# Two GpSimd sums placed behind both normalisations of a step, and unread TensorE products around the last two second norms, in a four-block sequence model

## What is computed

```python
# layers 0, 1 and 3; layer 1 has a causal mask and no bias on q, k, v
h = layernorm(x) * (1 + scale1) + shift1             # "first norm"
x = x + gate1 * (softmax(q(h) k(h).T / 4) v(h) @ Wo + bo)
h = layernorm(x) * (1 + scale2) + shift2             # "second norm"
x = x + gate2 * (gelu(h @ W1 + b1) @ W2 + b2)
# layer 2: attention, then a second norm added to its own input, no MLP
x = x + (softmax(q k.T) v / 16) @ Wp + bp
x = x + gamma * layernorm(x) + beta
```

## Time and profile before

| | us |
|---|---|
| median of 3 runs | 1178.21 (1176.1 to 1182.58) |
| the profiled execution | 1179.05 |
| its span, first to last instruction | 1177.3 |
| PE busy | 1073.8 (91%) |
| PEld busy | 852.4 (72%) |
| DVE busy | 779.3 (66%) |
| ACT busy | 574.3 (49%) |
| POOL busy | 174.9 (15%) |
| mean granted TensorE clock, full = 1 | 0.981 |

### The profile page before, as it was taken

How to read it: one execution, slowest core, us unless ns; L and a number is a source line. 1 busy time by engine, 2 the same in 40 slices (tenths; PEclk the granted TensorE clock), 3 DMA queues, 4 the chain that set the end, 5 groups by cost and what they waited for, 6 DMA issues and landing times.

```text
span 1177.3 us, 21434 instructions
## 1 busy us (share of the span) xinstructions
PE 1073.8 (91%) x7540; PEld 852.4 (72%) x7540; DVE 779.3 (66%) x2091; ACT 574.3 (49%) x1140; POOL 174.9 (15%) x288
## 2 busy tenths in 40 slices
PE   5799999999999999999999978888888999999895
PEld 4667777788787787877888755555556787877664
DVE  4476667776677666777666677766768766667622
ACT  4245565554553445544456444444445545655441
POOL 3011011110113101101101101111114110101100
PEclk9799999999999999999999999999999999999988
DMA  7732333222345223331233433333434123332200
GB/s 235 252 113 65 92 109 109 81 63 72 109 154 188 67 83 109 109 103 56 70 106 112 136 110 109 109 109 109 132 130 145 56 75 108 117 117 67 78 2 17
DMA packets 102714, 123.20 MB, mean 105 GB/s; under 512 B 8992, under 2 KB 96032, under 8 KB 101600
## 3 DMA queue, kind: packets, MB, share of 16 engines
q1 hardware_dynamic: 102048, 121.73, 33.1%
q10 hardware_dynamic: 576, 0.30, 0.1%
HBM read 85.16 MB, written 35.78 MB: 103 GB/s over the span
## 4 chain that ended last, share of the span: by engine, by line
PE 64%; DVE 13%; DMA 9%; ACT 4%; issue 3%; SPq 3%; POOL 1%; ACTq 1%; DVEq 0%; POOLq 0%
PE dense L1175 13%; PE o_banks L1252 8%; PE s_bank L1199 8%; PE dense L1161 8%; DMA q_stack<-max_t 6%; PE st_bank L1236 5%; PE o_banks L1135 4%; PE dense L1106 4%; DVE xn L773 3%; PE o_banks L1121 3%; DVE neg_max L801 3%; PE o_banks L1085 2%; PE o_banks L1260 2%; DMA k_stack<-qk_dram 2%; ACT probs L609 2%
## 5 line engine op out<-in xcount | busy, mean ns | idle before, releaser
L609 ACT ACTIVATE probs<-st_bank 128x512 f32<-128x512 f32 (+1 forms) x512 | 264.1, 568 | 173.2 <-PE st_bank L1236 121.4
L801 DVE TENSOR_REDUCE neg_max<-s_bank 128x2 f32<-128x512 f32 x384 | 255.6, 684 | 103.1 <-PE s_bank L1199 100.7
L1199 PE MATMUL s_bank<-k_stack,q_stack 96*128 96x256 f32 (+1 forms) x1024 | 234.3, 320 | 19.1 <-DMA k_stack<-qk_dram 10.7
L1199 PEld LDWEIGHTS s_bank<-k_stack,q_stack 96*128 96x128 f32 x1024 | 170.9, 194 | 60.3 <-DVE neg_max L801 16.7
L1175 PE MATMUL dense<-w_sb,hid 128*128 128x256 f32 x768 | 204.9, 381 | 0.0
L1236 PE MATMUL st_bank<-q_stack,k_stack 98*128 98x512 f32 x384 | 153.9, 474 | 13.3 <-DMA q_stack<-max_t 10.6
L444 POOL TENSOR_TENSOR veps<-mv,eps_c 128x2 f32<-128x2 f32 x65 | 14.3, 220 | 958.2 <-DVE mv L767 891.5
L1175 PEld LDWEIGHTS dense<-w_sb,hid 128*128 128x128 f32 x768 | 128.9, 189 | 9.6 <-issue 0.4
L597 ACT ACTIVATE hid<-dense,vec 128x256 f32<-128x256 f32 x192 | 80.6, 471 | 107.9 <-PE dense L1161 107.9
L1252 PE MATMUL o_banks<-probs,v_aug 128*32 128x256 f32 (+1 forms) x2048 | 123.0, 382 | 10.1 <-DVE xg L840 5.8
L1106 PE MATMUL dense<-ht,w_sb 128*128 128x256 f32 x512 | 127.3, 388 | 3.9 <-ACT ht L551 1.3
(11 more groups left out here) (124 smaller groups left out, 1467.9 us busy)
## 6 DMA issues: line engine op xcount, KB each, us to landing
q_stack<-qk_dram SPq DMA_DIRECT2D x192, 128.0 KB, 2.9
k_stack<-qk_dram SPq DMA_DIRECT2D x96, 256.0 KB, 4.1
par_sb<-par_dram SPq DMA_DIRECT2D x32, 512.0 KB, 5.3
qk_dram<-q_hi SPq DMA_DIRECT2D x32, 256.0 KB, 2.1
qk_dram<-q_lo SPq DMA_DIRECT2D x32, 256.0 KB, 2.1
qk_dram<-k_hi SPq DMA_DIRECT2D x32, 256.0 KB, 2.1
qk_dram<-k_lo SPq DMA_DIRECT2D x32, 256.0 KB, 2.1
w_sb<-w SPq DMA_DIRECT2D x3, 1280.0 KB, 7.6
```

The costliest lines, as they stand in the source:

```text
L609: nc.scalar.activation(probs[p % 4][:, kt, :, q0:N], src, ACT.Exp, scale=SCORE_SCALE[l]).then_inc(p_sb, 1)
L801: nc.vector.tensor_reduce(neg_max[:, qt, 2 * p:2 * p + 2], split3(bank[:]), AX.X, ALU.max, negate=True).then_inc(s_max, 1)
L1199: ins = mm(bank[:, e * N:e * N + k1], q_stack[g.par][0:KB, 2 * p + e, qt * P:(qt + 1) * P].bitcast(F32R), k_stack[g.par][0:KB, p, 0:k1].bi ...
```

## The change

Three edits.

1. On GpSimd, `addend(c, 1, xg2)` no longer follows `pick(c, 1, ...)`. Both sums now stand behind `power(n, 0, ...)` and behind waits for the first norm of n and the second norm of c. The wait for `par_sb` stands ahead of the sums, no longer ahead of `power(n, 0)`.
2. On TensorE, a new function `unread` issues n products of a bf16 identity by a bf16 mask (128x256) into a PSUM bank that nobody reads at that time. 20 of them stand ahead of `ht2_t` in step 31.
3. After the last projection, 44 of them stand ahead of `ht2_t(last, None)` and 14 behind it.

The computed result is the same.

```diff
                     if c.layer != 2:
                         pick(c, 1, mod2_now)
 
-                    addend(c, 1, xg2)
                     if g.reg is None and g.off % B == 1 and g.layer > 0 and HAS_MLP[g.layer]:
                         split_w1(g.layer)
-                wait(pool, par_ld, g.count(16, 16))
                 if n.exists:
+
                     power(n, 0, ln1_mv, ln1_veps, ln1_rstd)
-                else:
+                    wait(pool, xn1_done, n.count(1, 1))
+                if c.exists:
+                    wait(pool, xn2_done, c.count(1, 1))
+                    wait(pool, par_ld, g.count(16, 16))
+                    addend(c, 1, xg2)
                     wait(pool, xg2, c.count(1, 1))
-                    wait(pool, xn2_done, c.count(1, 1))
+                else:
+                    wait(pool, par_ld, g.count(16, 16))
                 addend(g, 0, xg1)
@@
                     score_t(g, 2)
+                    if not a.exists:
+                        unread(dense[0], 20)
                     ht2_t(c, a)
@@
+            def unread(bank, n):
+
+                for _ in range(n):
+                    mm(bank[:, 0:2 * P], ident_b[:], mask_k[:], start=True, stop=True)
@@
             for t in range(T):
                 projection(last, t)
+            unread(dense[0], 44)
             ht2_t(last, None)
+            wait(pe, prod2, STEPS - 1)
+            unread(dense[1], 14)
             for i in range(FT // 2):
```

More of the change, by code:

```diff
@@ L490, in step @@
                         pick(c, 1, mod2_now)
-                    addend(c, 1, xg2)
                     if g.reg is None and g.off % B == 1 and g.layer > 0 and HAS_MLP[g.layer]:
                         split_w1(g.layer)
-                wait(pool, par_ld, g.count(16, 16))
                 if n.exists:
                     power(n, 0, ln1_mv, ln1_veps, ln1_rstd)
-                else:
-                    wait(pool, xg2, c.count(1, 1))
-                    wait(pool, xn2_done, c.count(1, 1))
+                    wait(pool, xn1_done, n.count(1, 1))
[3 more added lines that the diff above has]
+                    addend(c, 1, xg2)
+                    wait(pool, xg2, c.count(1, 1))
+                else:
+                    wait(pool, par_ld, g.count(16, 16))
                 addend(g, 0, xg1)
```

## The result

| 20 runs of each, in turn on one chip | us |
|---|---|
| the changed kernel | 1174.27 (1166.4 to 1184.39) |
| the kernel before | 1182.3 (1176.1 to 1188.55) |
| ratio | 0.9927 [0.9906, 0.9949] |
| profiled execution after, its span | 1172.1, 1170.3 |

One of the 20 runs of the changed kernel (1184.39, at a mean clock of 0.934) was in a slower state and is left out of the ratio. The change makes the kernel faster by 0.7%, some 8.6 us. Forecast were 15.0 us and 1164.0; the measured 1174.27 lies above the range. Some 3 us of the miss in absolute time are the base: the profiled execution before (1179.05) and the three runs beside it (1178.21) lie low in what 20 runs of the same kernel show (1182.3). Against the forecast's own base the range ended at a ratio of 0.993 (1171 to 1179.05), just above the measured one. The rest is the effect itself.

A forecast was written before the change was run, and what follows sets the result against it. TensorE, busy 91%, was taken to lose most waiting at the second norm's transposes, where VectorE collides with GpSimd's sum. Gains 9.8 + 3.4 + 1.8 = 15.0 us from 1179.05 gave 1164.0, range 1157 to 1171.

The forecast's parts named there:

- the slower rival: Sums behind the first norm hold up the row maxima, VectorE about 1.4 us late in 24 steps: 1198 us; chance 0.03.
- the one in which the change has no effect: The second norm is slow for another reason and keeps 1.74 us; only the clock is won, 4.8 us: 1174.2; chance 0.05.
- TensorE therefore gains about 0.40 + 0.22 = 0.6 us: Per unmasked step: chain to `modulate2` moves 0.40 us, plus 0.22 slack between `ht_lo` and `mlp_up`, where TensorE then waits.
- The 1.3 us for the stack load: Layer 1: the stack load behind `k_lo` moves 0.27 us, not 0.53, so five masked steps give back 1.3 us.
- The sum of the middle: Edit 1: 7.8 us unmasked steps, 3.7 masked, less 1.3 stack load, less 0.4 steps 9 and 25: 9.8 us.
- Most is given back: Rival: maxima, stack loads and max rows' DMA set the pace; 4 us of the middle left, 9.2 in all: 1170; chance 0.12.
- With bias no stack wait shows in most steps: The argument given against the rival in which only 4 us of the middle are left.
- that can only help: GpSimd's wait for `par_sb` no longer stands ahead of `power(n, 0)`; costed at nothing.
- What was costed at nothing elsewhere: Layer 2's norm is covered by other waits (0.8 us in 8 steps without cover); later sums and `pick` harm nobody.
- Edit 2, forecast 3.4 us: Step 31: 20 products keep the clock full; 0.4 earlier start, 0.5 transposes, 0.8 `mlp_up` and scores, 1.7 values.
- The clock falls: Rival: in step 31 the clock falls despite 20 products; middle and end hold, 12.0 us won: 1167; chance 0.15.
- Edit 3, forecast 1.8 us: Last sequence: 44 and 14 products keep the clock full; `mlp_up` saves 1.4 us, transposes 0.46; 0 if it falls.

The follow-up runs named there:

- sums_only: The kernel before with edit 1 alone, without the products of edits 2 and 3; ratio to the kernel before 0.9951.
- only_second_norm: The changed kernel, but only the sum for c moved, behind the second norm; the sum for g stays colliding with the first norm; 0.9949 against the kernel before.
- both_again: The changed kernel unaltered, run again for a second profile and ratio; 0.9953 against the kernel before.
- split_early: The changed kernel with `split_w1` ahead of `power(c, 1)` in steps 9 and 25, last sum behind the last norm, 37 products for 44; 0.9947 against the kernel before.
- max_rows_on_act: The changed kernel with the second half's max rows issued from ScalarE's queue, `par_sb` load at its old place; 0.9951 against the kernel before.
- par_behind_max: The changed kernel with SyncE's `par_sb` load behind the second half's max rows instead of ahead; 1155.22 us, 0.9755 against the kernel before.
- products_only: The kernel before with edits 2 and 3 alone, sums at their old place; ratio to the kernel before 0.9969.

## Why the forecast was wrong

- **The mechanism at the norm was right.** The norm fell from 1.74 to 0.74 us, the wait at the transposes from 22.7 to 2.6 us, and reductions beside a sum did not grow (55 of them in the trace after, 0.69 us each), so the slower rival is out. So is the one in which the change has no effect.
- **"TensorE therefore gains about 0.40 + 0.22 = 0.6 us"** was right for its place: at `values(g, 0)` the 13 steps without the mask were 6.95 us ahead together (forecast 7.8), the 7 with it 3.57 (forecast 3.7). Of the 0.22 us counted as slack, 0.06 were none: `mlp_up` starts that much behind the end of `ht_lo` even where it waits for it (1082.70 and 1082.76). The 1.3 us for the stack load did not come in this profile; the wait for `k_stack` even fell a little, from 8 places to 5. In that of `sums_only` the masked steps lost 0.9 us at this place. Steps 9 and 25 won nothing in the norm (2.0 us before, 2.1 after, forecast 2.0 to 2.4).
- **The sum of the middle failed, "7.8 + 3.7 - 1.3 - 0.4 = 9.8 us".** It ends at `mlp_up` and takes what is won there as won for the step. I had listed what is late next in the chain of the norm, and not followed TensorE to the next thing that does not move with it. That was the DMA of the max rows, 10.6 us in 17 places before, in plain sight in the total waits. 6.3 us of the middle were left. It is the rival "Most is given back", which named maxima, stack loads and the max rows' DMA; in this profile only the last did it. "With bias no stack wait shows in most steps" spoke against the stack loads, but says nothing on the max rows, and with that I gave it 0.12.
- **The moved wait for `par_sb`, "that can only help",** was costed at nothing, and the direction stands. With the load early it had little to give: in the kernel before it ended last ahead of `power(n, 0)` in five places, at most 0.4 us later than the variance would have, and in the changed kernel GpSimd waits for the load nowhere. The load's late place needs it: without it that place is slower by 0.9%, with it faster by 1%. The wait moved alone, with the load early, was not tried.
- **What was costed at nothing elsewhere** (layer 2, the later sums, `pick`) shows no cost beyond the variation between executions. For the first norm see `only_second_norm`.
- **Edit 2, forecast 3.4 us,** was 3.3 in the changed kernel's profile, where the clock held. It held in six of nine profiled kernels with the products; in `both_again`, `split_early` and `max_rows_on_act` it fell, and step 31 won 1.8 us. That is the rival "The clock falls", which the forecast had as a case for good, and which came in one execution of the changed kernel and not in the other.
- **Edit 3, forecast 1.8 us,** was 1.7: the last sequence, from 32.00 to 30.29. The products ran at 0.11 us each, where 0.12 were forecast.

Sum: 15.0 forecast, less 3.5 in the middle, less half a us on average for the clock, is 11.0. The measured effect is 8.6 (5.5 in `both_again`, with an interval up to 9.5). The step-by-step sum of one execution does not explain the last 2 us; they are of the size by which the start and layer 2 vary.

**The better version** is the changed kernel with the load of `par_sb` behind the max rows: 0.9755 and 0.9785 against the kernel before, where the change alone has 0.9927.

## What to carry to other kernels

Follow a gain past the point where it arises to the next release that does not move with it, a DMA above all, and look for that release in the total waits before adding up. A small transfer that an engine waits for belongs ahead of the large one that nobody needs yet, and before it is moved, look which engine waits for the large one ahead of work that does not read it. Edits that bring little or even cost something alone (edit 1 0.9951, the load moved 1.0094) can be worth 2% together (0.98), so try them crosswise.

## What the runs showed of the hardware

**A small transfer behind a large one was late on either of two queues.** The trace has the DMA packets. In us behind the step's start, means of the 20 regular steps (on SyncE's queue the rows' packets are taken to be the last 16 of 1 KB ahead of `score_t`):

| run | rows issued | their 16 packets | packets of `par_sb` | `score_t` |
|---|---|---|---|---|
| changed kernel | 19.15 to 20.56 | 21.54 to 22.55 | 19.33 to 22.41 | 23.24 |
| `par_behind_max` | 19.18 to 20.60 | 20.58 to 21.46 | 21.76 to 24.18 | 22.41 |
| `max_rows_on_act` | 19.15 to 20.45 | 21.12 to 22.66 | 19.25 to 22.53 | 23.46 |

The last packet of the rows moves as late as the last of the large load, on the other engine's queue too, and 1.1 to 1.2 us later than without the load ahead. The Trainium skill, page "DMA: Bandwidth & Descriptors", section "Queues, rings and completion order", says that SyncE and ScalarE each own a ring on the same 16 DMA engines, which take packets from the rings in turn, and that the write to the semaphore lands only after every earlier write of its DMA engine, across its queues. The rule on the semaphore alone would make the count late and not the data. Here the data themselves came late: on ScalarE's queue each packet of 1 KB was followed at once by one of 4 bytes, in step 29 all between 1058.16 and 1060.02. Why rows on a ring of their own did not get their turn sooner was not found.

**The clock fell after the same idle time in one execution and held in another.** The windows below (stretch in us, its length, then PE, PEld, DVE, ACT, POOL busy with counts, granted clock, DMA share and GB/s) stand around the gap before `mlp_up` in step 31, behind 20 products and the transposes. In the changed kernel, where TensorE had waited 1.87 us:

```profile
1112.50:1118.00 5.50, 4.24 (x32) 3.42 (x31) 2.81 (x8) 3.29 (x8) 3.58 (x5) 1.00 0.00 0
1118.00:1124.00 6.00, 5.39 (x60) 4.33 (x61) 4.12 (x8) 2.23 (x4) 0.00 (x0) 1.00 0.01 3
```

In `both_again`, the same program, where it had waited 1.88 us:

```profile
1115.00:1116.50 1.50, 0.00 (x0) 0.00 (x0) 1.47 (x3) 1.48 (x3) 0.46 (x1) 1.00 0.00 0
1116.50:1118.50 2.00, 1.98 (x8) 1.78 (x8) 1.17 (x2) 0.79 (x2) 0.00 (x0) 0.50 0.00 0
1118.50:1121.00 2.50, 2.50 (x33) 1.14 (x32) 0.69 (x1) 0.00 (x0) 0.00 (x0) 0.72 0.03 7
```

There the clock went to the lower of its two levels (0.50, 1.2 GHz) at the first matmul behind the gap and came back within the window of 0.72. Over the nine profiled kernels with the products, it fell in three of the five where TensorE had waited 1.87 to 1.94 us there, and in none of the four where it had waited 1.41 or 1.42 (`products_only` and the three with the load behind). What decides among the five was not found.

**Small VectorE instructions are held as well.** A copy on 8 partitions took 1.35 us beside the split and 0.27 without it, five times as long. It ended 0.15 us behind its partner on GpSimd (368.08 and 367.93), as short as it is by itself. So what the norm had shown for two large instructions was seen here, once, for one of 8x256 too.
